# Eight-stage decoder on one core: group-wise key waits, one reordered GpSimd turn, statistics one step later, and a peeled pass of the last loop

## The reference, cut to what matters

```python
x = x + _L0_attn_ref(_layernorm(x), ...)    # 16 heads of 64
x = x + _L0_xattn_ref(_layernorm(x), ctx_1024, mask, ...)
x = x + _L0_ffn_ref(_layernorm(x), ...)     # 16 experts, top 2, 2 shared
x = x + _L1_attn_ref(_layernorm(x), ...)    # 16 heads of 8, relative positions
x = x + _L1_xattn_ref(_layernorm(x), ctx_1024, ...)
x = x + _L1_ffn_ref(_layernorm(x), ...)     # 8 experts, all computed, top 2 weighted
```

```python
# _L1_attn_ref: scores of query l against key r, 16 heads of 8
attn = jnp.einsum('bhld,bhrd->bhlr', q, k) * scale
rel  = jnp.einsum('bhld,lrd->bhlr', q, pos_emb) * scale
attn = jax.nn.softmax(attn + rel, axis=-1)
# _L1_ffn_ref: every expert for every token, weighted by the router
fuse_BTEF  = jax.nn.silu(gating_BTEF) * jnp.einsum('BTD,EDF->BTEF', x, kernel_up_EDF)
down_BTED  = jnp.einsum('BTEF,EFD->BTED', fuse_BTEF, kernel_down_EFD)
out_BTD    = jnp.einsum('BTED,BTE->BTD', down_BTED, full_weights_BTE)
```

## Time and profile before

| what | value |
| --- | --- |
| median of the runs (3) | 1363.59 us |
| profiled execution, its own time | 1360.92 us |
| its span | 1358.6 us |
| TensorE busy | 1240.3 us (91%) |
| VectorE busy | 984.2 us (72%) |
| ScalarE busy | 711.7 us (52%) |
| GpSimd busy | 650.1 us (48%) |
| mean granted TensorE clock | 0.962 of full speed |

### The profile page before, as it was taken

One profiled execution on the slowest core, in us unless ns is written; L12 is line 12 of the kernel. 1 busy time (PEld: TensorE's weight loads), 2 busy tenths in 40 slices (PEclk: granted clock), 3 DMA queues, 4 the chain that ended last, 5 costly groups with the idle time before them and its releaser, 6 DMA issues.

```text
span 1358.6 us, 29396 instructions
## 1 busy us (share of the span) xinstructions
PE 1240.3 (91%) x10886; PEld 913.6 (67%) x10886; DVE 984.2 (72%) x2403; ACT 711.7 (52%) x1473; POOL 650.1 (48%) x786
## 2 busy tenths in 40 slices
PE   7999999999999989861849998999999999899998
PEld 5667667766776756540339766777777777677887
DVE  5888897788779778768425466687877879776554
ACT  4666656766666645620113345666656666533221
POOL 3555556555655631130456468876654755401110
PEclk9999999999999999975879999999999999999999
DMA  5241000000000020000014132321220211000001
GB/s 179 59 125 32 1 1 2 1 1 2 1 1 1 1 71 2 1 1 0 5 49 115 45 63 85 87 59 25 44 51 20 57 36 31 1 1 1 0 0 31
DMA packets 77048, 43.88 MB, mean 32 GB/s; under 512 B 26138, under 2 KB 71787, under 8 KB 76919
## 3 DMA queue, kind: packets, MB, share of 16 engines
q1 hardware_dynamic: 72438, 38.59, 11.0%
q10 hardware_dynamic: 2432, 2.28, 0.6%
q0 software_dynamic: 2048, 1.27, 0.4%
HBM read 21.91 MB, written 10.49 MB: 24 GB/s over the span
## 4 chain that ended last, share of the span: by engine, by line
PE 65%; DVE 17%; ACT 6%; issue 4%; POOL 4%; DMA 1%; SPq 1%; ACTq 0%; DVEq 0%; POOLq 0%
PE psum L1737 8%; PE psum L1314 7%; PE psum L1299 6%; PE psum L1846 6%; PE psum L1289 6%; PE psum L1749 4%; PE psum L1857 4%; PE psum L1721 4%; PE psum L1728 3%; ACT arena L937 2%; PE psum L1265 2%; POOL xs_rows L703 2%; PE psum L1564 2%; DVE arena L2258 2%; DVE negmax L2533 1%
## 5 line engine op out<-in xcount | busy, mean ns | idle before, releaser
L645 POOL TENSOR_TENSOR arena<-arena,rden 128x512 f32<-128x512 f32 x256 | 260.6, 1042 | 214.9 <-DVE rden L1992 214.8
L937 ACT ACTIVATE arena<-psum,negmax 128x512 f32<-128x512 f32 x256 | 175.1, 694 | 150.9 <-DVE negmax L1983 124.0
L2533 DVE TENSOR_REDUCE negmax<-psum 128x1 f32<-128x512 f32 x256 | 164.6, 685 | 49.3 <-PE psum L1728 44.2
L1983 DVE TENSOR_REDUCE negmax<-psum 128x1 f32<-128x512 f32 x256 | 168.1, 681 | 40.2 <-PE psum L1289 39.1
L1299 PEld LDWEIGHTS psum<-cst,arena 128*128 128x128 f32 x1024 | 112.6, 140 | 47.2 <-issue 46.5
L1299 PE MATMUL psum<-cst,arena 128*128 128x128 f32 x1024 | 139.3, 277 | 4.4 <-DVE arena L1978 0.8
L1289 PE MATMUL psum<-a_qk 64*128 64x512 f32 x768 | 106.0, 408 | 2.5 <-DVE a_qk L2001 2.5
L1846 PE MATMUL psum<-f_h,f_w 128*128 128x512 f32 x384 | 100.8, 411 | 5.1 <-DVE arena L2631 5.1
L1721 PE MATMUL psum<-a_kstack,a_qblk 96*128 96x512 f32 x256 | 96.0, 457 | 5.1 <-DMA a_kstack<-a_klo 3.9
L1195 ACT ACTIVATE arena<-psum 128x512 f32<-128x512 f32 x64 | 38.1, 597 | 106.2 <-PE psum L1846 106.1
L1289 PEld LDWEIGHTS psum<-a_qk 64*128 64x128 f32 x768 | 67.2, 184 | 39.1 <-issue 24.2
(11 more groups left out here) (361 smaller groups left out, 2845.2 us busy)
## 6 DMA issues: line engine op xcount, KB each, us to landing
w<-in_ew SPq DMA_DIRECT2D x2, 2048.0 KB, 8.7
a_kstack<-a_khi SPq DMA_DIRECT2D x64, 64.0 KB, 2.0
xs_rows<-f SPq DMA_DIRECT2D x3, 1024.0 KB, 5.3
ys_rows<-wqkv SPq DMA_DIRECT2D x8, 384.0 KB, 3.0
arena<-xs_rows SPq DMA_DIRECT2D x7, 384.0 KB, 3.8
a_kstack<-a_klo SPq DMA_DIRECT2D x32, 64.0 KB, 1.9
a_kstack<-a_khi SPq DMA_DIRECT2D x64, 32.0 KB
a_qstack<-a_qhi SPq DMA_DIRECT2D x121, 16.0 KB, 2.2
```

Source lines behind the costliest of these rows:

```text
L645: pool.tensor_tensor(a0_p[u % 4], a0_p[u % 4], rden[:, u:u + 1].broadcast_to([P, SEQ]), ALU.mult).then_inc(a0_norm, 1)
L937: act.activation(a0_p[u % 4], bank[u % 4][:, :], ACT.Exp, bias=negmax[:, u:u + 1], accum_out=den[:, u:u + 1]).then_inc(a0_exp, 1)
L1983: dve.tensor_reduce(negmax[:, u:u + 1], bank[u % 4][:, :], AX.X, ALU.max, negate=True).then_inc(a0_max, 1)
L2533: dve.tensor_reduce(negmax[:, n % 8:n % 8 + 1], bank[n % 4][:, :], AX.X, ALU.max, negate=True).then_inc(a1_max, 1)
```

## The change

There are four edits.

1. The keys of all turns are counted by group: groups 0, 1 and 2 on `a1_kfirst`, `setup` and `a1_emb`, group 3 on `a1_kin` (turn 0 has its groups 2 and 3 there). TensorE waits for a group at p = 0, 2, 4 and 6 of every turn; `high_k` and `low_k` wait for the four groups of the turn before.
2. In turn 1, GpSimd's `add_experts(1)` stands behind `stage_v(1)` and `low_k(2)` instead of ahead of them.
3. The statistics of sequence 1 on VectorE are taken at p = 5 and 6 of turn 1 instead of 4 and 5, and `guest_scale` follows p = 6 instead of 5.
4. In the last sublayer VectorE's pair i = 1 is taken out of the loop and written out, with `f1_hid(1, 0)` and `f1_hid(1, 1)` ahead of `add(0, 6)`, and `f1_hid(1, 2)` ahead of `add(0, 7)`. The other engines keep their loop over pairs 1 to 3.

```diff
         def keys_of_group(it, g):
-            own = ((a1_kfirst, 48), (setup, 6 + 48)), ((a1_kfirst, 96), (setup, 6 + 96), (a1_emb, 3 + 96))
-            return own[it][g] if it < 2 and g < len(own[it]) else keys_stacked(it)
+            if g == 0:
+                return a1_kfirst, 48 * it + 48
+            if g == 1:
+                return setup, 6 + 48 * it + 48
+            if g == 2 and it:
+                return a1_emb, 3 + 48 * it + 48
+            return a1_kin[it % 2], 48 * (it // 2) + (48 if it % 2 else 96)
...
-        SCALE_AT = {(it, 5): ("pre", b) for it, b in PRE_NORM.items()}
+        SCALE_AT = {(it, 6 if it == 1 else 5): ("pre", b) for it, b in PRE_NORM.items()}
...
@@ low_k on GpSimd, and the same in high_k on ScalarE
                 if it:
-                    pool.wait_ge(*keys_stacked(it - 1))
-                if it and it < 3:
-                    for g in range(4 if it == 2 else 2):
+                    for g in range(HQ):
                         pool.wait_ge(*keys_of_group(it - 1, g))
...
@@ GpSimd, the turns
                 gather_one(it, 1)
-                if it == 1:
-                    add_experts(1)
                 stage_v(it)
                 gather_one(it, 2)
                 if it < NT - 1:
                     low_k(it + 1)
+                if it == 1:
+                    add_experts(1)
                 gather_one(it, 3)
...
@@ TensorE, a1_scores
-                if p == 0 or it < 2 and p % 2 == 0:
+                if p % 2 == 0:
                     pe.wait_ge(*keys_of_group(it, p // 2))
...
@@ VectorE, pre_stats_of
-                if it in PRE_NORM and p in (4, 5):
-                    pre_stats(PRE_NORM[it], 2 * p - 8, 2 * p - 6)
+                late = it == 1
+                if it in PRE_NORM and p - late in (4, 5):
+                    pre_stats(PRE_NORM[it], 2 * (p - late) - 8, 2 * (p - late) - 6)
...
@@ VectorE, the last sublayer
             dve.wait_ge(g_chain, 500)
+            f1_hid(1, 0)
+            f1_hid(1, 1)
             add(0, 6)
+            f1_hid(1, 2)
             add(0, 7)
-            with dve.Fori(1, E1 // 2) as i:
+            f1_hid(1, 3)
+            add(1, 0)
+            for k in range(2, 8):
+                f1_hid(1, 2 * k)
+                f1_hid(1, 2 * k + 1)
+                add(1, k - 1)
+            add(1, 7)
+            with dve.Fori(2, E1 // 2) as i:
                 for k in range(8):
```

More of the change, by code:

```diff
@@ L394, in stacked @@
             return per_turn[it % 2], (it // 2 + 1) * STACK - (it + 1) % 2 * 96
-        def keys_stacked(it):
-            return a1_kin[it % 2], (it // 2 + 1) * STACK - (144 if it % 2 else 96)
         def keys_of_group(it, g):
-            own = ((a1_kfirst, 48), (setup, 6 + 48)), ((a1_kfirst, 96), (setup, 6 + 96), (a1_emb, 3 + 96))
-            return own[it][g] if it < 2 and g < len(own[it]) else keys_stacked(it)
+            if g == 0:
[5 more added lines that the diff above has]
+            return a1_kin[it % 2], 48 * (it // 2) + (48 if it % 2 else 96)
         def key_parts(it):
@@ L1119, in high_k @@
                     act.wait_ge(a1_klo, it)
-                    act.wait_ge(*keys_stacked(it - 1))
-                if it and it < 3:
-                    for g in range(4 if it == 2 else 2):
+                    for g in range(HQ):
                         act.wait_ge(*keys_of_group(it - 1, g))
```

## The result

The changed kernel takes 1356.83 us (median of 5 runs, 1355.02 to 1357.89) where the kernel before takes 1363.12 us in 5 runs (1357.92 to 1365.10). The ratio is 0.9963, with a 95% interval from 0.9945 to 0.9981: 6.3 us won at the medians, and between 2.6 and 7.5 us by the interval. The forecast was 6.0 us and 1357.0 us.

The account below looks back on a forecast made before the run. TensorE, busy 91% of the span, was taken as the bound, so only its gaps count. Terms 1.4 + 0 + 0.9 + 0 + 3.7 = 6.0 us gave a forecast of 1357.0 us, own range 1353 to 1361, wider 1350 to 1362.5.

Parts of the forecast that it names:

- the clock in turn 2: TensorE, turn 2: a gap comes back at the norm's transposes, so nothing won; bounds -1.8 and +1.8 us.
- Turn 1: TensorE, turn 1: VectorE's copy ends at 832.9 instead of 834.90, so the gap of 1.67 us goes.
- GpSimd's list and its successor: Turns 1 and 2: GpSimd's norm 1.4 us earlier, new TensorE wait of 3 to 4 us; gain 1.4 us.
- VectorE's scale: Scale for sequence 1's norm ready by 838.4, leaving 1.0 us of cover before GpSimd needs it at 839.4.
- The rival in which it comes late: Turn 2: late scale holds the norm at 846.3; gain 4.6 us, 1359.0 us; chance 0.15.
- the clock falls elsewhere: Two slow stretches at turn 2's gap, or the loop's start keeps its own: gain 2.4 to 4.2 us; chance 0.14.
- Turn 4: TensorE, turn 4: the key wait of 0.88 us goes; gain 0.9 us, between 0 and 0.9.
- The loop's start: Expert pair loop: TensorE goes on 1.9 us earlier and a 1.8 us slow stretch goes; together 3.7 us.
- The waits: Turns 2 to 15: 42 added waits on TensorE cost 0, at most 10.5 us.

Follow-up runs that it names:

- E2: Kernel before with edit 1 alone (keys awaited by group in all turns): 1362.01 us, 1.3 us faster, not to be told from none.
- E5: Changed kernel with the five TensorE steps that use sequence 1's norm one free step later: 1351.70 us, 10.2 us faster than before.
- e6: Changed kernel with one of turn 1's gathers on GpSimd moved behind the norm: 1355.66 us, 6.2 us faster than before.
- E3: Kernel before with edits 2 and 3 only: 1361.74 us, 1.6 us faster, unclear.
- e4: Changed kernel without edit 4 (edits 1 to 3 only): 1359.94 us, 3.4 us faster than before.
- e8: Changed kernel with VectorE's pair 1 written out but in the loop's old order: 1359.78 us, 2.1 us faster than before.
- e10: Changed kernel with 160 more always satisfied waits on TensorE: 1359.34 us, 2.7 us faster than before.
- e9: Changed kernel with four matmuls of no use ahead of the norm's transposes in turn 2: 1354.23 us, 7.8 us faster than before.
- e1: Kernel before with edit 4 alone: 1360.16 us, 3.2 us faster.
- e11: Kernel before with edit 4 and sequence 1's norm used one free step later, without edits 1 to 3: 1361.69 us, no change.

## Why the prediction was right

**Where the gain sits.** It was forecast as 2.3 us in the turns and 3.7 us at the loop. The runs of the parts give 3.4 us (2.3 to 4.8) and 3.2 us (1.1 to 4.9). The sum was right, and the split is within what they can tell. That the sum met the measurement to 0.3 us is in part luck: the term for the clock in turn 2 was wrong, and not all that edits 1 to 3 gave has a term (both below).

**Turn 1.** Right. The gap of 1.67 us behind the copy is gone in the profile after. E2, which keeps the order of turn 1, still has 1.59. No run has edit 3 without edit 2, so which of the two removes it rests on the rows of VectorE.

**GpSimd's list and its successor.** Right in kind and nearly in size: 1.6 us instead of 1.4 for the norm's start, and a new wait of 4.52 us instead of 3 to 4. A turn's values are named here after the turn in whose step p = 2 they stand. From the values of turn 1 to the transposes (823.46 to 846.67 before, 826.67 to 848.84 after) 1.0 us is won. The values' rows in turns 1 and 2, of before and of after:

```profile
823.46 1.95 PE L1749 MATMUL psum<-arena,w 128*32 128x128 f32 x64
...
851.92 1.96 PE L1749 MATMUL psum<-arena,w 128*32 128x128 f32 x64
```
```profile
826.67 1.96 PE L1746 MATMUL psum<-arena,w 128*32 128x128 f32 x64
...
855.44 1.95 PE L1746 MATMUL psum<-arena,w 128*32 128x128 f32 x64
```

E5 shows by removal that this wait, and not the work of the other engines, held the rest.

**VectorE's scale.** Right: 2.0 us of cover, 1.0 forecast (1.1 us in e6, whose norm starts earlier). The rival in which it comes late did not occur.

**The clock in turn 2.** This is the step that failed: the prediction counted nothing for the clock, since one gap would take the place of another. After the transposes the change needs 855.44 - 848.84 = 6.6 us to the values of turn 2, before 851.92 - 846.67 = 5.25 us, and those 1.35 us take back the 1.0 that the norm gave. In the profile turn 2 as a whole wins nothing (28.8 us from values to values, 28.5 before). A second low stretch follows at 864 us, where before has none; from the values of turn 2 to those at p = 6 it takes 16.28 us instead of 14.64. E3, e4, e6 and e8, which have the norm's gap too, also have this one; e10 has the gap and not this one; e9, with the gap filled, has neither. The premise of the rival "the clock falls elsewhere" (two slow stretches instead of one behind a longer gap) was right; its price, a gain of only 2.4 to 4.2 us, did not come out. The length of a gap does not settle what follows it: in e8 the matmuls behind 2.53 us of idle time take 5.49 us, before they took 4.35 us behind 2.55 us.

**Turn 4.** Right for the profile: 0.88 us gone. It is a low reading, though: where the old wait stands in other kernels it is 1.61 (e1), 0.90 (e3) and 2.52 us (e11).

**The loop's start.** 3.0 us in the profile and 3.2 in e1, where 3.7 was forecast. The clock part held: 4.35 and 2.06 us have become 3.06 and 1.78, which is 1.57 us of the 1.84. The other part is 0.4 us short. The first silu ends at about 1240.14, yet the product that needs it starts at 1240.58; this chain of after names the time between:

```profile
1240.18 0.40 issue
1240.58 0.70 DVE arena L2629
```

What VectorE does in it no run shows.

**The waits.** Right: 0.001 us each in e10's profile.

**What stays open.** The profiles do not show where the 3.4 us of edits 1 to 3 come from. From the values at p = 6 of turn 0 to those at p = 6 of turn 4, where these edits act, the profile before needs 99.84 us (812.11 to 911.95) and the profile after 99.62 us (816.22 to 915.84). That is 0.2 us. Another 3.1 us of the profile's gain lie where nothing was edited. Around 923 and 1019 us before has a low stretch of the clock and the change has none. The values on either side of the first, of before, of the change, and of e8, whose instructions are the change's up to the last sublayer:

```profile
911.95 1.95 PE L1749 MATMUL psum<-arena,w 128*32 128x128 f32 x64
...
928.04 1.95 PE L1749 MATMUL psum<-arena,w 128*32 128x128 f32 x64
```
```profile
915.84 1.96 PE L1746 MATMUL psum<-arena,w 128*32 128x128 f32 x64
...
930.39 1.95 PE L1746 MATMUL psum<-arena,w 128*32 128x128 f32 x64
```
```profile
916.17 1.95 PE L1746 MATMUL psum<-arena,w 128*32 128x128 f32 x64
...
932.39 1.95 PE L1746 MATMUL psum<-arena,w 128*32 128x128 f32 x64
```

They are 16.09, 14.55 and 16.22 us apart, and the second place gives the same three times. So these 3.1 us are an accident of the profiled executions and not of the edits. The medians owe nothing to such accidents as far as the clocks tell: the mean over all runs is 0.9596 for the change and 0.9599 for e4, and 0.9592 to 0.9603 for before in the three groups. The gain of edits 1 to 3 at the medians thus stands, but its place is not shown. Higher readings of turn 4's wait can carry some of it.

## What to carry to other kernels

Before counting a removed wait, look for the next thing that its engine needs, and for when that is ready: here 4.7 us of gaps were removed and turned into a wait for a norm, until its use was moved one free step later. Edits that were worth some 3 us alone were worth some 10 us with the one that took away the wait behind them, and that one was worth nothing that shows alone. A gap of a few us in front of matmuls costs more than its length if the clock falls with it, and that also holds for a gap that has only been moved. Before two profiles are subtracted, look for slow stretches at places that no edit touches.

## What was not expected of the hardware

A matmul of no use on 128 x 512 float32 with a plain identity took 0.88 us, twice what the rows of other 512-column matmuls suggested (0.41 to 0.47 us), and showed as two instructions. Around the gap of 4.5 us the mean granted clock was 0.57 over 8 us, around the one of 3.03 us before 0.72 over 6 us. The clock also fell with no idle time ahead of it: before, TensorE is busy from 916.12 on with 16 matmuls, every second of which has one row (L1647 and L1649), and the clock is at 0.50 from 919.5 to 922.9; behind the same 16 in the change it stays at 1.00. Between the end of a silu and the VectorE product that waits for it lay 0.4 us at the loop's start; some rounds earlier it was 0.1 us (a silu ends at 1230.97, its product starts at 1231.08).
